# The first feed-forward pair step placed ahead of the last attention step, in a patch-embedding, attention and feed-forward kernel

## What is computed

```python
h = h + attn(layernorm(h))        # 12 heads of 64, 4-bit fake-quantised operands
h = h + ffn(layernorm(h))

def bitlinear(x, w, g):           # used twice by ffn: 192 -> 2*512, then 512 -> 192
    x_norm = rmsnorm(x, g)
    scale = 127.0 / max(max(abs(x_norm), axis=-1), 1e-5)      # one scale for each row
    x_q = clip(round(x_norm * scale), -128, 127) / scale
    w_q = ternary(w)
    return einsum('bsd,od->bso', x_q, w_q)

def ffn(x, ...):
    up, gate = split(bitlinear(x, w_in, g_in))
    return bitlinear(silu(gate) * up, w_out, g_out)
```

## Time and profile before

| | |
|---|---|
| median of 3 runs | 1294.4 us (1293.33 to 1295.1) |
| profiled execution: its own time | 1294.41 us |
| its span in the trace | 1292.4 us |
| busy in the span | PE 1131.2, DVE 1089.9, ACT 937.0, POOL 471.7 us |
| mean granted clock of PE | 0.902 of full speed |

### The profile page before, as it was taken

How to read it: one execution, slowest core, us unless ns; L and a number is a source line. 1 busy time by engine, 2 the same in 40 slices (tenths; PEclk the granted TensorE clock), 3 DMA queues, 4 the chain that set the end, 5 groups by cost and what they waited for, 6 DMA issues and landing times.

```text
span 1292.4 us, 31971 instructions
## 1 busy us (share of the span) xinstructions
PE 1131.2 (88%) x10782; PEld 698.4 (54%) x10782; DVE 1089.9 (84%) x1980; ACT 937.0 (73%) x1877; POOL 471.7 (36%) x540
## 2 busy tenths in 40 slices
PE   7999995999999999999999999998357777777776
PEld 6999994345555555555555555555224344444443
DVE  6656777299999999999999999999479999999896
ACT  0000000999999999999999999997168888888886
POOL 5544534002222222222212222222256666666664
PEclk9999997899999999999999999999567777777776
DMA  8999994245555665555556555555313233233222
GB/s 283 327 281 285 306 284 150 81 133 149 142 146 153 143 141 142 140 139 139 140 144 148 146 146 150 138 138 133 69 50 86 86 89 88 79 91 88 87 71 77
DMA packets 158360, 187.65 MB, mean 145 GB/s; under 512 B 42865, under 2 KB 119745, under 8 KB 158017
## 3 DMA queue, kind: packets, MB, share of 16 engines
q1 hardware_dynamic: 90656, 138.99, 33.5%
q10 hardware_dynamic: 52224, 37.37, 9.5%
q0 software_dynamic: 15360, 9.70, 8.3%
HBM read 143.06 MB, written 36.12 MB: 139 GB/s over the span
## 4 chain that ended last, share of the span: by engine, by line
PE 71%; ACT 8%; DVE 7%; issue 6%; DMA 3%; ACTq 2%; POOL 2%; SPq 0%; DVEq 0%; POOLq 0%
PE psum L1134 19%; PE psum L1194 12%; PE psum L1068 10%; PE psum L1181 8%; PE psum L1164 7%; PE psum L1225 7%; PE psum L1147 6%; ACT yi L609 2%; PE psum L1246 2%; ACT big L602 2%; DVE big L1043 2%; ACT ysq L629 1%; ACT zi L617 1%; POOL pt L723 1%; PE psum L1236 1%
## 5 line engine op out<-in xcount | busy, mean ns | idle before, releaser
L708 POOL DMA_DIRECT2D h_res<-att x128 | 144.6, 1191 | 571.0 <-ACT att L546 561.9
L920 DVE TENSOR_TENSOR pi<-big 128x2364 int16<-128x2364 f32 (+1 forms) x128 | 334.6, 2614 | 5.6 <-DMA big<-z_row 5.5
L570 ACT ACTIVATE big<-psum 128x788 f32<-128x788 f32 (+1 forms) x384 | 317.0, 828 | 1.4 <-DVE pi L920 1.4
L1068 PE MATMUL psum<-big 128*128 128x192 f32 (+1 forms) x1128 | 182.5, 326 | 1.0 <-DMA big<-xt 1.0
L1068 PEld LDWEIGHTS psum<-big 128*128 128x128 f32 (+1 forms) x1128 | 180.6, 188 | 2.1 <-DVE big L806 1.3
L1134 PE MATMUL psum<-xT,w1b 128*128 128x394 bf16 x768 | 164.9, 338 | 18.1 <-DMA xT<-x_int 16.1
L532 ACT ACTIVATE qki<-psum 128x394 int16<-128x394 f32 x384 | 172.2, 512 | 2.0 <-DVE qkb L796 1.1
L1225 PE MATMUL psum<-winb,zT 96*128 96x512 bf16 (+1 forms) x396 | 145.2, 532 | 32.1 <-DVE big L1043 31.2
L1194 PE MATMUL psum<-big,sa_hot 128*32 128x197 f32 (+1 forms) x3072 | 168.2, 336 | 0.0
L532 ACT ACT_TABLE_LOAD x1 | 1.3, 1283 | 226.9 <-PE psum L1134 226.9
L742 POOL TENSOR_TENSOR big<-big,goutb 128x512 f32<-128x512 f32 (+1 forms) x99 | 123.8, 1271 | 77.1 <-DVE big L1043 77.1
(11 more groups left out here) (102 smaller groups left out, 1741.2 us busy)
## 6 DMA issues: line engine op xcount, KB each, us to landing
big<-z_row SPq DMA_DIRECT2D x192, 394.0 KB, 5.1
big<-xt SPq DMA_DIRECT2D x98, 384.0 KB, 4.4
tin<-h_res SPq DMA_DIRECT2D x49, 192.0 KB, 2.4
tres<-h_res ACTq DMA_DIRECT2D x49, 192.0 KB, 2.5
out<-oo ACTq DMA_DIRECT2D x49, 192.0 KB, 2.6
h_res<-big ACTq DMA_DIRECT2D x78, 96.0 KB, 4.3
h_res<-att POOLq DMA_DIRECT2D x64, 96.0 KB, 3.4
x_int<-big ACTq DMA_DIRECT2D x93, 64.0 KB, 4.2
```

Source lines behind the costliest of these rows:

```text
L570: act.activation(ex[0:r, tri, t, 4 * g:4 * g + 4, :].rearrange("p (a h) n -> p a h n", a=2), psum[0:r, 2 * t:2 * t + 2, 0:2 * N] .rearrang ...
L708: pool.dma_start(h_res[bass.ds(b - 4, 1), t0:t0 + r, :].rearrange("a n d -> (a n) d"), att[0:r, par, t, :], accum_op=ALU.add).then_inc(s_a ...
L920: v.tensor_tensor(pi[0:r, t, :, 0:N], ex[0:r, it, t, :, :], zb[0:r, ip, :, :], ALU.mult).then_inc(s_pi, 1)
L1068: last = mm(psum[p0:p0 + r, s, 0:D], xring[:, s, c * 128 + p0:c * 128 + p0 + r], weight_of(cls, c), start=(c == 0), stop=(c == KC - 1))
```

## The change

`over_images` now calls pair step 0 between image step 66 and image step 67 on every engine, and `over_pairs` starts at step 1. SP loads the pair t+1 in pair step t, and pairs 0 and 1 in step 0. The waits for all images at the start of the third stage go: a load waits for the images that its rows lie in when its pair number is 0 to 3 and for all images above (`wait_added`); ACT waits for all images ahead of its residual loads in the written-out steps 4 to 9. On PE the wait for all quantised weights (`s_wq`) now stands ahead of the images, and on DVE two small copies (`wdeq4`) too. The short description of the change also names a ring of four for the dequantising factors; the diff has no edit of a buffer, and `pt` keeps its two.

```diff
@@ over_pairs
-            for t in range(first):
+            for t in range(1, first):
@@ 
-        def over_images(eng, step):
-            for b in range(-2, B + 4):
-                step(b, b % 2, b % 3)
+        def over_images(image_step, pair_step):
+            for b in range(-2, B + 3):
+                image_step(b, b % 2, b % 3)
+            pair_step(0, 0)
+            image_step(B + 3, (B + 3) % 2, (B + 3) % 3)
+
+        def wait_added(eng, t):
+            last = (256 * (t + 1) - 1) // N if t < 4 else B - 1
+            for p in range(2):
+                wait(eng, s_added[p], 32 * ((last - p) // 2 + 1))
@@ SP
-            over_images(sp, image_step)
-            for p in range(2):
-                sp.wait_ge(s_added[p], 32 * (B // 2))
             def pair_step(t, par):
-                if at := pair_of(t)(0):
-                    r, n = at
-                    wait_apart(sp, s_t["zc"], t - 1)
-                    sp.dma_start(tin[0:r, par, 0:n, :], pair_rows(h_att, t, r, n)).then_inc(s_t3[par], 16)
+                pair, oth = pair_of(t), 1 - par
+                if at := pair(-1):
+                    r, n = at
+                    if isinstance(t, int):
+                        wait_added(sp, t + 1)
+                    wait_apart(sp, s_t["zc"], t)
+                    sp.dma_start(tin[0:r, oth, 0:n, :], pair_rows(h_att, t + 1, r, n)).then_inc(s_t3[oth], 16)
+
+            def first_step(t, par):
+                wait_added(sp, 0)
+                sp.dma_start(tin[:, 0, :, :], pair_rows(h_att, 0, 128, 2)).then_inc(s_t3[0], 16)
+                pair_step(t, par)
+
+            over_images(image_step, first_step)
@@ ACT (its own call of over_images moves behind pair_step)
                 if at := pair(4):
                     r, n = at
+                    if isinstance(t, int):
+                        wait_added(act, NPAIR - 1)
                     act.dma_start(tres[0:r, par, 0:n, :], pair_rows(h_att, t - 4, r, n)).then_inc(s_t3b[par], 16)
...
-            for p in range(2):
-                act.wait_ge(s_added[p], 32 * (B // 2))
+            over_images(image_step, pair_step)
@@ PE
-            over_images(pe, image_step)
-            pe.wait_ge(evac["y"], B)
...
             pe.wait_ge(s_wq, 4)
+            over_images(image_step, pair_step)
+            pe.wait_ge(evac["y"], B)
             over_pairs(pe, pair_step)
```

More of the change, by code:

```diff
@@ L578, in _ @@
             act.wait_ge(s_stage_free, 4)
-            over_images(act, image_step)
             def pair_step(t, par):
@@ L709, in image_step @@
                                        att[0:r, par, t, :], accum_op=ALU.add).then_inc(s_added[par], 16)
-            over_images(pool, image_step)
             def pair_step(t, par):
@@ L956, in image_step @@
                     normalise(b - 2, par, (tri + 1) % 3, 1)
-            over_images(dve, image_step)
             for k in range(2):
```

## The result

| | before | changed |
|---|---|---|
| median | 1294.75 us (1293.33 to 1295.91, 4 runs) | 1286.74 us (1285.88 to 1290.22, 4 runs) |
| ratio of the medians | | 0.9944, 95% interval 0.9922 to 0.9965 |
| profiled execution, own time | 1294.41 us | 1290.22 us |
| its span | 1292.4 us | 1288.3 us |

The kernel is faster by some 8 us (5 to 10 by the interval). Forecast were 1284.3 us and 10.1 us of gain; the time lies in the range 1282.0 to 1287.6. The profiled execution of the changed kernel is the slowest of its four, so its span is read piece by piece and not as one difference.

The account below looks back on a forecast made before the run. The prediction took a serial chain of waits between attention and the third stage as the bound the edit touches. A gain of 10.1 us, with all other terms 0, gave 1294.4 - 10.1 = 1284.3 us, range 1282.0 to 1287.6.

Parts of the forecast that it names:

- What bounds the seam: Between attention and third stage: single steps in a chain, no engine computing from 929.25 to 935.64 us.
- DVE's hole takes the step: DVE before image 63's weighted values: pair step 0, 2.2 us, fits in 5.20 us idle without delaying them.
- POOL as the queue to watch: 1/rms of pair 0 follows image 62's adds, done at 928.4; first `zi` at 930.2, gain 10.1 us.
- twice its longest: POOL's adds of image 63 stalled to 4.6 us: `zT` and first silu of pair 1 2.2 us late.
- Pair 1 has 0.6 us of slack: `zi` of pair 1 done at 935.3, PE's transposes want it at 935.9: cost 0, but narrowly.
- The broadcast of image 63: SP's zb transfer with two early loads queued behind it: cost taken as 0, at most 1.1 us.
- The clock: First hidden products on PE keep their lengths; 2.4 GHz back for two groups would gain 1.4 us more.
- rival 1: At the seam, clock back early or POOL's wait shorter: up to 1.4 and 0.9 us more gain; chance 0.16.
- What the first pair gains at the seam should be carried to the end unchanged: Third stage: only memory traffic depends on wall time, so the whole 10.1 us gain reaches the end.
- The signs: Expected in the changed profile: event times on DVE, POOL and PE, and third stage as long within a us.
- Rival 4: Third stage settles at 1.2 GHz every round: 45 groups x 0.69 = 31 us lost, 1315 us; chance 0.05.
- Weights' wait on PE and the copies on DVE: Moved ahead of the images: PE's wait met at 219.45, before `xT` at 226.02; DVE waits anyway; cost 0.

Follow-up runs that it names:

- the second measurement: The changed kernel with no further edit, measured once more against the kernel before: 1287.48 us, ratio 0.9928.

## Why the prediction was right

By its own steps:

- *What bounds the seam, and that DVE's hole takes the step:* right. Step 0 took 2.26 us in the hole of 5.20, `ob` of image 63 was not late (12.72 us behind L932, as before), and no engine waits for the adds at the seam any more. The early loads by themselves gave 6.4 us and the move 4.2.
- *POOL as the queue to watch:* right, and the term was a little too large. The prediction had the adds of image 62 at 1.78 us (1.77), then 0.41 + 0.78 us for 1/rms. The addition took 0.19 and the power 0.72. The 0.41 us of the row used stood behind 5.34 us of idle time; why it was longer is not shown. `zi` came 3.90 us behind `ob`, where 930.2 - 925.86 = 4.3 was forecast. So the seam gave 10.6 us instead of 10.1. Taking POOL out of the way gave 0.67 us more, where the prediction had bounded it with 0.9. The upper end of the range rests on POOL stalled for "twice its longest", put at 4.6 us; twice 2.42 is 4.84, so this bound would have been some 2.4 us and not 2.2.
- *Pair 1 has 0.6 us of slack:* right. `zi` of pair 1 was done 0.5 us ahead of PE's transposes of it (938.42 and 938.94). In the changed kernel the transposes of pair 1 start right behind the hidden products of pair 0, 3.39 us after these start, as before (935.55 to 938.94; before 942.62 to 946.00).
- *The broadcast of image 63:* cost 0 was right within the scatter of a few tenths of a us, tested with three times the bytes. That the Trainium skill's page "DMA: Bandwidth & Descriptors", section "Queues, rings and completion order", has the descriptors of a ring taken in order agrees with it: 7.58 us with 1152 KB behind, 6.12 to 7.58 without.
- *The clock:* rival 1 did not come true in its part on the clock; of its part on POOL, up to 0.9 us, some 0.5 came. The first two groups took 3.60 and 3.57 us as before, at the level of 1.2 GHz, although PE's idle time ahead of them shrank from 12.6 to 2.0 us. The third took 3.57, as in three of the four profiles of the kernel before; its 2.88 in the first was the exception. The granted clock had been 0.50 from 905 us on in both kernels, long before the gap. The Trainium skill's advice in "TensorE: Matmul & The Clock Gate", section "Why this matters for your kernels", was weighed as a possible gain; this seam doesn't test it, since the clock was down before the gap, and closing most of the gap did not bring 2.4 GHz back earlier.
- *"What the first pair gains at the seam should be carried to the end unchanged":* right for the mechanism, too sure for one execution. The difference of the medians is 8.0 us, and 8.4 in the second measurement, against 10.1 forecast. The step that is off is the sum made against a single profiled execution, as if all stages but the seam had a fixed length. They scatter: the start of the second stage by 5.4 us over the eight profiles (222.9 to 228.3), the third stage by 3.5. The profile that I worked from had the shortest third stage of its kernel. The range had no term for this scatter, nor for the cost of some 1 us that may lie in the third stage; that 1286.74 lies inside it is in part luck, and the second median, 1287.48, is only 0.1 us inside.
- *The signs:* most were set as absolute instants or lengths, and several of these failed in the first profile without the mechanism being wrong. DVE's normalisation came at 916.67 and not 913.14, the second stage started at 228.3 and not 226.0, and the third stage was 2.9 us longer, not within 1. From its issue the broadcast took 6.73 us to the normalisation, against 7.37, so it was not held up. A sign for an edit at a seam should be a distance from an event beside it.
- *Rival 4, the slower rhythm:* it exists, but small. Rounds at 1.2 GHz last about 7.35 us and rounds at 2.4 GHz about 6.5 to 6.9. The price of a cold group against a mixed one was put at 0.69 us a round; measured it is 0.5 (7.34 against 6.80). Which rounds are cold changes from one execution to the next in either kernel.
- *Weights' wait on PE and the copies on DVE:* no cost seen. PE waits for `xT` just as long, 15.97 us, and the second stage starts no later in the mean of ten profiles.

## What to carry to other kernels

Where two stages meet, ask for each wait which data it is for: one wait for "all images" held a load of the first two. Giving each early load its own condition was worth more than half of the gain. When a step is moved into a hole of the busy engine, place its small helpers on the slow side engine by that engine's own queue; two instructions of 0.9 us together cost 3 us of waiting behind the issue of two transfers when they stood on the wrong side of them. And make the forecast for an edit at a seam from the seam, but its uncertainty from several profiles of the whole.

## What the runs showed of the hardware

- Six loads, 1152 KB, queued on SP's queue behind a broadcast of 3 x 394 KB, did not delay it beyond the scatter (7.58 us from its issue to the engine that needs it, 6.12 to 7.58 with none behind, 6.73 to 8.07 with two).
- TensorE's granted clock went from 0.72 to 0.81 over the third stage when each pair got two more matmuls of 512 columns, and the time did not rise; it fell by some 2 to 3 us if anything. I had put up to 0.9 us per round on the additions as a loss.
- POOL's addition of 128x2 numbers took 0.41 us after a pause of 3.9 us or more and 0.19 right behind other work; the power after it took 0.78 and 0.72. In the kernel before the second addition, 0.90 us after the power, took 0.41 too, and the third, after 1.08 us, 0.19, so the pause alone does not explain it.
- In the last attention steps TensorE's clock was at the 1.2 GHz level (0.50 from 905 us on; PE busy 4.46 of the 10 us to 915 in the kernel before), and the first two groups of hidden products ran at this level in all fourteen profiles, whether PE had been idle for 12.6 us ahead of them or for 0.6.
